# Batches 0 and 1 of a router: row scatters begun singly behind the selects of units 12, 13 and 15

## The reference, cut to what matters

```python
x = x + attention(layernorm(x))      # 16 heads of 8, rotary, causal softmax
x = x + experts(layernorm(x))        # 8 experts, the best 2 of each token
x = x + spectral(layernorm(x))       # a long convolution, gates and a feed-forward part
x = x + experts(layernorm(x))        # the same weights again
```

```python
logits = x @ Wr.T
vals, idx = top_k(softmax(logits), 2)
gate = one_hot(idx) weighted by vals / vals.sum()
y_e = silu(x @ W1[e].T) @ W2[e].T
out = sum over e of gate[e] * y_e
```

## Time and profile before

| | |
|---|---|
| timed runs, median (range) | 631.68 us (628.78 to 633.11) |
| span of the profiled execution | 658.8 us |
| busy share of the span | PE 78%, DVE 57%, POOL 48%, ACT 38% |
| row scatters (L461), both expert layers | 64, 62.6 us of POOL |
| selects (L1331) | 64, 38.9 us of POOL |

### The profile page before, as it was taken

The page is one execution under the profiler, slowest core; times in us unless marked ns, Lnnn a source line. Parts: engine busy times, 40 slices in busy tenths (PEclk is TensorE's granted clock), DMA queues, the critical chain, the costliest instruction groups (busy, mean ns, idle before and its releaser), DMA issues. The chain is left out here.

```text
span 658.8 us, 12208 instructions
## 1 busy us (share of the span) xinstructions
PE 513.1 (78%) x3527; PEld 359.1 (54%) x3528; DVE 378.8 (57%) x1248; ACT 250.2 (38%) x518; POOL 318.9 (48%) x373
## 2 busy tenths in 40 slices
PE   2998999999898569569950598999799427689950
PEld 1444555555454259569950344545467327689950
DVE  3879888878968355234434549632947843234423
ACT  1323877676667323134463222101132202234433
POOL 1454479542665554624443953243423755434543
PEclk9999999999998788789995689999999659789995
DMA  6176031233221124234423000000000112222225
GB/s 184 48 215 181 23 102 59 83 112 119 66 65 37 47 83 116 84 84 118 117 85 93 1 0 1 0 0 1 0 1 14 44 57 62 59 77 67 68 66 161
DMA packets 46520, 46.11 MB, mean 70 GB/s; under 512 B 8661, under 2 KB 39952, under 8 KB 46320
## 3 DMA queue, kind: packets, MB, share of 16 engines
q1 hardware_dynamic: 37968, 31.48, 17.3%
q0 software_dynamic: 4544, 9.35, 4.2%
q10 hardware_dynamic: 3952, 4.59, 2.2%
HBM read 31.68 MB, written 15.12 MB: 71 GB/s over the span
## 5 line engine op out<-in xcount | busy, mean ns | idle before, releaser
L1243 ACT ACTIVATE store<-ps 128x512 f32<-128x512 f32 x160 | 90.3, 595 | 48.4 <-PE ps L814 39.9
L1034 DVE TENSOR_REDUCE at_mx<-ps 128x1 f32<-128x512 f32 (+1 forms) x128 | 72.8, 615 | 15.8 <-PE ps L801 15.3
L461 POOL DMA_INDIRECT expert_rows<-r_rows,r_sloti x64 | 62.6, 978 | 31.4 <-issue 18.1
L799 PE MATMUL ps<-at_hats 72*128 72x512 bf16 (+3 forms) x256 | 67.7, 302 | 4.5 <-DVE at_mx L1034 2.7
L597 POOL DMA_INDIRECT expert_results<-store x39 | 37.6, 963 | 51.6 <-issue 19.9
L814 PE MATMUL ps<-at_hats 74*128 74x512 bf16 (+3 forms) x256 | 60.8, 301 | 1.4 <-ACT store L1243 1.1
L1331 POOL TENSOR_SCALAR_AFFINE_SELECT store<-store 128x512 f32<-128x512 f32 x64 | 38.9, 634 | 46.8 <-ACT store L1243 46.8
L597 POOL DMA_INDIRECT expert_results<-at_vall x39 | 37.5, 961 | 49.6 <-DVE at_vall L539 28.1
L831 PE MATMUL ps<-store,at_vext 128*32 128x128 f32 (+3 forms) x512 | 49.2, 461 | 6.7 <-ACT at_oT_more L1211 6.6
L582 PE MATMUL ps<-moe_w,store 128*128 x312 | 45.6, 294 | 7.0 <-ACT store L553 3.6
L582 PE MATMUL ps<-moe_w,at_hats 128*128 x312 | 44.5, 290 | 7.4 <-issue 7.4
(11 more groups left out here) (313 smaller groups left out, 1058.1 us busy)
## 6 DMA issues: line engine op xcount, KB each, us to landing
at_hats<-parts SPq DMA_DIRECT2D x48, 96.0 KB
at_hats<-parts SPq DMA_DIRECT2D x16, 288.0 KB
moe_w<-moe_w_dram SPq DMA_DIRECT2D x8, 512.0 KB, 4.4
store<-ssm_tables_dram SPq DMA_DIRECT2D x35, 86.0 KB
at_vall<-expert_rows SPq DMA_DIRECT2D x39, 64.5 KB
store<-expert_rows SPq DMA_DIRECT2D x39, 64.5 KB
at_hats<-expert_results SPq DMA_DIRECT2D x8, 256.0 KB, 4.8
sm_gates<-expert_results SPq DMA_DIRECT2D x8, 256.0 KB, 5.4
```

The lines of the kernel that those rows point to most:

```text
L461: pool.indirect_dma_start(self.xs_dram[:, :], bass.IndirectOffsetOnAxis(self.sloti[:, n, k:k + 1], 0), self.rows[:, k, n, :], None).then_i ...
L799: pe.matmul(bankA(n)[:, col:col + (t + 1) * P], hatq[0:MROW, slot, h, t * P:(t + 1) * P], hatk[0:MROW, slot, h, 0:(t + 1) * P], start=True ...
L1034: m = dve.tensor_reduce(mx[:, u % 2, t, h:h + 1], bankA(n)[:, 0:(t + 1) * P], AX.X, ALU.max)
L1243: act.activation(pt[:, u % 2, j // 2, S * (j % 2):S * (j % 2 + 1)], bankB(n), ACT.Exp).then_inc(s_e, 1)
```

## The change

The four scatters behind the selects of units 11, 12 and 14 (all four selects first, then the four scatters) move to units 12, 13 and 15, and there one scatter follows each select. Batch 1's second copies (k = 1) stood ahead of unit 15's selects and now stand behind the loop, ahead of batch 2's. The number of scatters stays the same. POOL's calls of `scatter` gain a wait each, since `scatter` waits for its semaphores at each call; these are met by then.

```diff
-        SCATTERS = {11: (0, 0), 12: (0, 1), 14: (1, 0)}
+        SCATTERS = {12: (0, 0), 13: (0, 1), 15: (1, 0)}
...
                 if u == 14:
                     router.inverse_root(pool, 2)
-                if u == 15:
-                    router.scatter(pool, 1, 1)
...
                     pool.affine_select(out=own, in_=own, compare_op=ALU.is_ge, fill=0.0, base=0,
                                        pattern=[[0, HG], [1, P]], channel_multiplier=-1).then_inc(s_causal, 1)
+                    if u in SCATTERS:
+                        router.scatter(pool, *SCATTERS[u], range(t, t + 1))
...
-                if u in SCATTERS:
-                    router.scatter(pool, *SCATTERS[u])
...
+            router.scatter(pool, 1, 1)
             router.scatter(pool, 2, 0)
             router.scatter(pool, 2, 1)
```

## The result

The changed kernel has a median of 632.46 us (629.32 to 635.68, 20 runs) against 630.68 us (626.22 to 634.10, 20 runs) for the kernel before, run beside it. The ratio is 1.0044 with a 95% interval of [1.0022, 1.0065]: 1.4 to 4.1 us slower, 2.8 in the middle. This ratio is estimated over the fast executions of both kernels and is not the quotient of the two medians, which is 1.0028 (1.8 us). The forecast was 634.8 us, 3.1 above its base.

The account below looks back on a forecast made before the run. No single engine was taken to bound the kernel. The late first tile put the projection's end at 238.1, plus 6.9 to transposes at 245.0 against 241.7 to 241.9 before: 631.7 + 3.1 = 634.8 us, range 628.5 to 638.5.

Parts of the forecast that it names:

- Late signals only in the one traced execution: PE's signals seem late in rows of scatters; the 27.1 us of extra span laid to the trace; forecast case, chance 0.50.
- rivals 2 and 3: Timed runs pay late signals: 2, alternating pays none, -2.3 us, chance 0.17; 3, row of twelve holds projection's signal, +0.9, 0.20.
- The changed kernel's schedule up to the first tile: Unit 15 and first expert tile: batch 1's last scatter 7.4 us later, 6 us slack used up, PE waits 6 us.
- From the first tile to the end of the projection: PE's stretch, 5.7 us now; bounds 3.7 to 5.7, taken as 4.1 because the 2.0 us weight-copy wait goes.
- The kernel before without late signals: Base reckoning: unit 15's values at 225.0, first tile 228.9, projection 234.6, batch 3's transposes 241.7 to 241.9.
- Units 12 and 13: Later selects cost nothing, with 5.4 and 2.7 us cover; addition of batch 2's attention 0.7 to 0.9 us later.
- What binds the transposes: Batch 3: before, the root behind batch 2's scatters, done 240.4; after, DVE's addition plus 6.9 us, transposes at 245.0.
- Rival 4: Loads inside long scatter rows are slow, second expert tile 4.3 us behind the first: +6.1, 637.8 us, chance 0.10.
- Rival 5: DVE weight copy delays a scatter, at most 0.43 us twice: no added shift; 638.3 us by the page's rule; chance 0.03.

Follow-up runs that it names:

- the filled kernel: Changed kernel plus nine unread 512-column matmuls on PE between batch 3's attention transposes and the first expert tile: ratio 1.0050, +3.1 us against the kernel before.
- the kernel with the fourth scatter moved: Kernel before with only batch 0's scatters singly behind selects of units 12 and 13, unit 13's fourth behind POOL's addition of batch 2's attention: one traced execution, 631.14 us.
- batch 1's half: Kernel before with only batch 1's scatters changed: first copies singly behind unit 15's selects, second copies behind the last select: ratio 1.0042, +2.6 us.
- the second copies moved alone: Kernel before with only batch 1's second copies moved behind unit 15's selects, other scatters in bursts where they were: ratio 0.9935, -4.1 us.
- the load latest of all: Kernel before with batch 1's second copies moved behind batch 2's first ones, all else unchanged: ratio 1.0134, +8.4 us.
- the one with the root between: Kernel before, batch 1's second copies behind unit 15's selects, batch 3's fifth round and projection before the first tiles, its root between batch 2's copies: 0.9959, -2.6 us.

## Why the prediction was right, point by point

- **Late signals only in the one traced execution: right.** The second trace of the kernel before has a span of 630.5 us and none of them. That takes rivals 2 and 3 away, which both needed them.
- **The changed kernel's schedule up to the first tile: right within 0.8 us.** Unit 15's selects at 217.2 (forecast 217.5), values done at 223.9 (224.1), last of batch 1's scatters at 228.6 (228.7), first load at 231.9 (232.1), first tile at 233.85 (234.0), PE's wait 5.8 (6). The forecasts were made on a trace in which unit 12's first select lay at 188.35, against 188.85 here; measured from it, all of these came 0.6 to 0.8 earlier than forecast.
- **From the first tile to the end of the projection: mis-sized.** I took 4.1 us, near the lower bound; it was 5.0 (233.85 to 236.97 + 1.91). The waited-for weight copy did go, as argued, but L571 and L870 ran at half the clock: 1.92 and 1.91 us against 1.13 and 1.06 in the second trace before. The prediction had no term for the clock. It also misread its own trace: what it calls a wait of 2.0 for the weight copy is 0.55 us of idle time there, and for 4.6 us of that stretch of 5.7 PE was busy, at a granted clock of 0.71. Without any wait the stretch takes 2.9 us at full clock (the filled kernel) and 5.0 at half, so 4.1 is neither.
- **The kernel before without late signals: mis-sized.** I had the values at 225.0, so 36.7 behind unit 12's first select, and the tile at 40.6; they are at 38.2 and 43.0. I took 3.64 us for the values; they are 4.50 at a granted clock of 0.50 after PE's wait of 5.59, and unit 15's selects are 1.0 us earlier than traced, not 1.4. Batch 2's scatters, which wait for slots that follow from the values, were forecast from 39.9 and began at 41.8. The transposes, with 53.4 to 53.6, came out only 1.0 early, because a second term was wrong the other way: from the end of the scatters to the end of the root I took 2.4 us, a traced distance that holds 0.69 us of idle time, and it is 1.4. Both sides were too early at the transposes, the changed one by 0.3 us and the one before by 1.0, so the difference shrank from 3.1 to 2.4 there.
- **Units 12 and 13: right but for 0.3 us.** Both units' last selects had their cover: PE waited for no select there. The addition of batch 2's attention is 0.9 late (0.7 to 0.9 said). DVE's operations beside it, not in the sum, added 0.3.
- **What binds the transposes: right.** Before, the root stood behind batch 2's scatters (243.30, no idle time) and DVE's rows of batch 3 waited for it. Now it waits for the moments (idle 1.3 us ahead of 241.03), but it no longer sets the time: it ends at 242.65, while DVE has `expert(2)` and its plan between the moments and the rows, and begins the rows at 244.59 without a wait for the root. The forecast's 6.9 us from the addition to the transposes holds that (6.9 measured).
- **Rival 4: fell.** PE took the second tile 1.1 us behind the first, not 4.3.
- **Rival 5: fell.** The scatter of 229.84 took 0.96 us beside the weight copy of 229.54, and that of 236.15 took 1.03 beside the copy of 235.92. What the traces show is the opposite direction: DVE's small operations with two inputs stretched beside POOL. The Trainium skill, "SBUF — State Buffer", section "SBUF: two separate sides", calls the port pair of VectorE and GpSimd a lock that the loser waits for; 2.56 us instead of 0.75 agrees with that, and so does the end of these operations behind POOL's addition in the kernel with the fourth scatter moved. 3,100 ns for a scatter appears nowhere here; the longest row scatter near the change took 1.25 us.
- **The size is partly luck.** The stretch behind the tile was 0.9 us short and the rest ahead of it 0.7 long, and on the side of the kernel before an error of 2.4 us at the tile was down to 1.0 at the transposes. What was right is the path: the late scatters, the late load, PE's wait, and the addition behind it.

The measured 2.8 us has 2.4 at the transposes. Behind them PE was at half the clock once more, for one tile (granted 0.57 from 245.80 to 249.80, after 0.98 from 239 to 245): from the transposes to the logits of batch 3 it took 4.0 us (245.81 to 249.80) against 2.4 (246.00 to 248.36), 1.6 more. The two traces so are 4.1 apart at the logits, at the upper end of the timed interval. Whether this second fall belongs to the change is not shown: it is there with batch 1's half (4.0) and with the second copies moved alone (3.8), which is a faster kernel, and not with the load latest of all (2.4).

The mechanism is shown by four comparisons: the half of the change that holds the late load has its cost; with the same alternation in unit 15 and the load 4.6 us earlier the kernel is 6.8 us faster; with the same selects and the load 10.4 us later it is 12.5 us slower; and taking the tail from behind the tile brings the transposes 3.2 forward. In nine of the eleven rows of the table the shift of the transposes against the kernel before lies within the interval of the time. What is not settled are the other two: the kernel with the second copies moved alone gains 4.1 us (2.3 at least) when its transposes gain 2.2 and its logits only 0.7, and the one with the root between gains 2.6 (4.3 at most) when its transposes gain 4.5.

## What to carry to other kernels

Of a queue that serves two consumers, ask of each move which consumer was late. Here the selects were late before and the row scatters after; alternating in unit 15 with batch 1's first copies left in POOL's gap of 4.3 us (and batch 0's as they were) took 4.2 us off, where the change added 2.8. And price a wait of PE with what follows it: here the stretch behind a 5.8 us wait took 2.2 us more than behind a busy PE (5.07 against 2.92).

## What was not expected of the hardware

Two traces of the same kernel, whose timed runs all lay between 625.0 and 637.6 us, had spans of 658.8 and 630.5 us. The longer one had waits without a releaser in rows of scatters, which the second trace doesn't have. A profile's span that doesn't fit the timed runs should be taken again before its waits are read.

DVE's small operations were stretched beside POOL's, more than POOL's beside theirs: four of 0.19 us each took 2.56 us beside a scatter and an addition and 1.86 where they began with the addition, while batch 2's scatters beside DVE's weight copies took at most 1.12 us against 0.96 (in the kernel with the second copies moved alone).
